# Applying the gate weight as expert results leave PSUM, and splitting the final adds between GpSimd and VectorE

## The reference, cut to what matters

```python
logits = x_flat @ gate_w.T
scores = jax.nn.softmax(logits, axis=-1)
_, topk_ids = jax.lax.top_k(scores, 2)                      # 8 experts, 2 per token
in_topk = jax.nn.one_hot(topk_ids, E, dtype=x.dtype).sum(axis=1)
w = scores * in_topk
gu = jnp.einsum('nh,eih->nei', x_flat, experts_gate_up)     # inner size 352
g, u = (gu[..., :I], gu[..., I:])
h = jax.nn.silu(g) * u
expert_out = jnp.einsum('nei,ehi->neh', h, experts_down)
out = jnp.einsum('neh,ne->nh', expert_out, w)
shared = jax.nn.silu(x_flat @ shared_gate_w.T) * (x_flat @ shared_up_w.T) @ shared_down_w.T
out = out + jax.nn.sigmoid(x_flat @ shared_expert_gate_w.T) * shared
x = x + jnp.tanh(g_ffn[1]) * out
```

## Time and profile before

| what | us |
|---|---|
| median of 3 runs | 1013.73 |
| lowest and highest run | 1010.68, 1014.83 |
| the profiled execution | 1013.72 |
| its span, first to last instruction | 1011.6 |
| TensorE busy | 944.7 |
| VectorE busy | 578.4 |
| ScalarE busy | 482.1 |
| GpSimd busy | 582.9 |

### The profile page before, as it was taken

One profiled execution on the slowest core, in us unless ns is written; L12 is line 12 of the kernel. 1 busy time (PEld: TensorE's weight loads), 2 busy tenths in 40 slices (PEclk: granted clock), 3 DMA queues, 4 the chain that ended last, 5 costly groups with the idle time before them and its releaser, 6 DMA issues. The chain is left out here.

```text
span 1011.6 us, 21397 instructions
## 1 busy us (share of the span) xinstructions
PE 944.7 (93%) x7715; PEld 537.0 (53%) x7716; DVE 578.4 (57%) x1698; ACT 482.1 (48%) x661; POOL 582.9 (58%) x620
## 2 busy tenths in 40 slices
PE   6989999999996997988999999998899999999994
PEld 3654444444464553644444444456456577777753
DVE  4867888888743123876888888837443222222226
ACT  2437777877843111326778788753301122222210
POOL 3468999999933900368999999961036222222210
PEclk9978999999997998998999999999999999999998
DMA  9581837364002160465243434111912212222143
GB/s 302 193 230 37 231 65 222 73 193 94 9 23 84 42 218 10 120 158 133 53 110 64 116 65 116 33 49 39 339 47 90 70 53 63 63 63 63 53 158 112
DMA packets 87988, 107.56 MB, mean 106 GB/s; under 512 B 10528, under 2 KB 70520, under 8 KB 87896
## 3 DMA queue, kind: packets, MB, share of 16 engines
q1 hardware_dynamic: 77192, 85.08, 30.4%
q0 software_dynamic: 4848, 14.70, 4.3%
q10 hardware_dynamic: 5856, 6.56, 2.1%
HBM read 76.92 MB, written 29.38 MB: 105 GB/s over the span
## 5 line engine op out<-in xcount | busy, mean ns | idle before, releaser
L616 ACT ACTIVATE pT<-ps 128x1024 f32<-128x1024 f32 x256 | 248.4, 1022 | 97.8 <-PE ps L488 97.5
L658 POOL TENSOR_TENSOR xT<-nmax,xT 128x512 f32<-128x512 f32 x192 | 195.5, 1040 | 20.6 <-DVE nmax L556 20.3
L658 POOL TENSOR_TENSOR s<-nmax,s 128x512 f32<-128x512 f32 x192 | 196.4, 1040 | 16.6 <-DVE nmax L556 12.4
L556 DVE CUSTOM_DVE_ANT_0 s<-ps,bias 128x512 f32<-128x512 f32 x256 | 166.1, 689 | 45.0 <-PE ps L475 43.8
L556 DVE CUSTOM_DVE_ANT_0 xT<-ps,bias 128x512 f32<-128x512 f32 x256 | 166.5, 689 | 41.6 <-PE ps L475 32.8
L475 PE MATMUL ps<-ks,qs 97*128 97x512 bf16 (+1 forms) x512 | 162.4, 397 | 10.7 <-DMA ks<-qk_scratch 4.5
L503 PE MATMUL ps<-pT,vq 128*32 128x512 f32 x1024 | 136.0, 608 | 2.4
L1186 POOL DMA_INDIRECT slots_out<-y,id x39 | 38.2, 980 | 128.6 <-DVE y L1513 128.6
L475 PEld LDWEIGHTS ps<-ks,qs 97*128 97x128 bf16 (+1 forms) x512 | 30.7, 98 | 130.3 <-DVE nmax L556 64.0
L1265 PE MATMUL ps<-gu,xgT 128*128 x312 | 98.8, 460 | 0.7 <-ACT xgT L1349 0.7
L488 PEld LDWEIGHTS ps<-ident,xT 64*128 64x128 f32 x2048 | 71.5, 143 | 29.2 <-issue 28.5
(11 more groups left out here) (173 smaller groups left out, 1179.5 us busy)
## 6 DMA issues: line engine op xcount, KB each, us to landing
bias<-in_bias SPq DMA_DIRECT2D x16, 1024.0 KB, 5.8
qk_scratch<-parts SPq DMA_DIRECT2D x64, 128.0 KB
qs<-qk_scratch SPq DMA_DIRECT2D x32, 192.0 KB, 3.4
ks<-qk_scratch SPq DMA_DIRECT2D x32, 192.0 KB, 4.0
gu<-in_gate_up SPq DMA_DIRECT2D x8, 704.0 KB, 9.7
slots_in<-zeros POOLq DMA_DIRECT2D x4, 1280.0 KB, 7.1
xg<-slots_in SPq DMA_DIRECT2D x39, 130.0 KB, 2.1
qk_scratch<-parts ACTq DMA_DIRECT2D x32, 128.0 KB
```

What stands on the lines that cost most here:

```text
L556: nc.vector.tensor_tensor_reduce(at.s[m % 4][:, qt, :], sb.ps[:, ring_bank(tile_place[u - 1 + hg * 64]), :], at.bias[:, j if per_head_bias ...
L616: nc.scalar.activation(at.pT[:, slot(m // HG, m % HG), 2 * half:2 * half + 2, :], sb.ps[:, 2 + 2 * half:4 + 2 * half, :], ACT.Exp).then_in ...
L658: nc.gpsimd.tensor_tensor(s, at.nmax[:, m % 4, qt:qt + 1].to_broadcast([P, S]), s, ALU.subtract).then_inc(pool_less_max, 1)
```

## The change

- **The weight travels with the row.** Before the scatters of each choice, GpSimd copies the 16 columns of m.w for that choice into word D + 1 of the rows of sb.tok. keep_id copies two words (row number and weight), and m.id grows to 128 x 4 x 2.
- **The weight is applied in keep_y.** The copy from PSUM becomes a tensor_scalar multiplication by the column m.id[:, u, 1].
- **GpSimd adds the two results of a batch.** Behind its last scatter it waits for both loads of a batch and adds sb.tok to yg in one tensor_tensor of 128x1024, for each of the four batches.
- **VectorE adds the sum in one operation.** expert_add is one tensor_tensor of 128x1024 per batch and waits for y_summed instead of the loads.
- **Order on VectorE.** expert_add of batch 0 now stands behind the first product of block (1,3) and that of batch 1 behind the second, ahead of the third product and of shared_add of (1,2). Batches 2 and 3 stay where they were. SP's stores wait for y_added of b + 1.

```diff
             for b in range(B):
-                sp.wait_ge(y_added, 2 * QT * (b + 1))
+                sp.wait_ge(y_added, b + 1)
                 sp.wait_ge(x_added, TT + QT * (b + 1))
...
                     nc.gpsimd.iota(sb.tok[:, :, D].bitcast(I32), pattern=[[P, TT]], base=N,
                                    channel_multiplier=1).then_inc(rows_named, 1)
-                    pool.wait_ge(rows_named, 3)
+                nc.gpsimd.tensor_copy(sb.tok[:, :, D + 1], m.w[:, c, :]).then_inc(rows_named, 1)
+                pool.wait_ge(rows_named, 3 + 2 * c)
                 for t in range(TT):
...
-                nc.gpsimd.tensor_copy(m.id[:, u:u + 1], m.xg[:, u, D:D + 1].bitcast(U32)).then_inc(id_kept, 1)
+                nc.gpsimd.tensor_copy(m.id[:, u, :], m.xg[:, u, D:D + 2].bitcast(U32)).then_inc(id_kept, 1)
...
             for it in range(ST // 4):
                 body(it, it == 0, it == ST // 4 - 1)
+            for b in range(B):
+                pool.wait_ge(y_loaded[b], 16 * 2)
+                rows = slice(QT * b, QT * (b + 1))
+                nc.gpsimd.tensor_tensor(m.yg[1][:, rows, :], m.yg[0][:, rows, 0:D], m.yg[1][:, rows, :],
+                                        ALU.add).then_inc(y_summed, 1)
...
-            def shared_prod(half, b):
+            def shared_prod(half, b, ready=0):
                 for i in range(SC):
...
                     nc.vector.tensor_tensor(hidden(half, b, i)[rows], m.g[rows, k % 2, :],
                                             sb.ps[rows, bank, :], ALU.mult).then_inc(s_prod, 1)
+                    if i < ready:
+                        expert_add(i)
...
                 dve.wait_ge(x_added, b * QT + QT)
-                dve.wait_ge(y_loaded[b], 16 * 2)
-                for c in range(2):
-                    for q in range(QT):
-                        t = b * QT + q
-                        if c == 1:
-                            dve.wait_ge(y_added, 2 * QT * b + q + 1)
-                        nc.vector.scalar_tensor_tensor(sb.x[:, t, :], m.yg[c][:, t, 0:D], m.w[:, c, t:t + 1],
-                                                       sb.x[:, t, :], ALU.mult, ALU.add).then_inc(y_added, 1)
+                dve.wait_ge(y_summed, b + 1)
+                rows = slice(QT * b, QT * (b + 1))
+                nc.vector.tensor_tensor(sb.x[:, rows, :], sb.x[:, rows, :], m.yg[1][:, rows, :],
+                                        ALU.add).then_inc(y_added, 1)
...
-                nc.vector.tensor_copy(m.y[:, u, :], sb.ps[:, 6 + u % 2, 0:D]).then_inc(y_kept, 1)
+                nc.vector.tensor_scalar(m.y[:, u, :], sb.ps[:, 6 + u % 2, 0:D], m.id[:, u, 1:2].bitcast(F32), None,
+                                        ALU.mult).then_inc(y_kept, 1)
...
             for n in range(1, len(late_blocks)):
-                shared_prod(*late_blocks[n])
+                half, b = late_blocks[n]
+                shared_prod(half, b, EARLY if n == 1 else 0)
                 shared_add(*late_blocks[n - 1])
-                if n == 1:
-                    for b in range(EARLY):
-                        expert_add(b)
                 dve.wait_ge(x_added, TT + (EARLY + n) * QT)
                 expert_add(EARLY + n - 1)
 
             expert_add(B - 1)
-            dve.wait_ge(y_added, 2 * TT)
+            dve.wait_ge(y_added, B)
             shared_add(*late_blocks[-1])
```

More of the change, by code:

```diff
@@ L1060, in mixture_phase @@
     id_kept, rows_named = sem("id_kept"), sem("rows_named")
-    y_added = sem("y_added")
+    y_summed, y_added = sem("y_summed"), sem("y_added")
     out_done = sem("out_done")
@@ L1186, in scatter_y @@
                 pool.indirect_dma_start(
-                    out=scr.ys, out_offset=bass.IndirectOffsetOnAxis(ap=m.id[:, u:u + 1], axis=0),
+                    out=scr.ys, out_offset=bass.IndirectOffsetOnAxis(ap=m.id[:, u, 0:1], axis=0),
                     in_=m.y[:, u, :], in_offset=None).then_inc(y_stored[u], 16)
@@ L1735, in build @@
                     m.xg = buf("xg", [P, 4, DW], F32)
-                    m.id = buf("id", [P, 4], U32)
+                    m.id = buf("id", [P, 4, 2], U32)
                     m.xgT = buf("xgT", [P, 2, DC, P], F32)
```

## The result

The changed kernel took 1002.18 us (median of 4 runs, 1000.65 to 1003.39) against 1012.53 before; the ratio is 0.9889, with a 95% interval of 0.9867 to 0.9911. The profiled execution took 1002.56 us, its span is 1000.8. Two later comparisons of the same pair gave 0.9896 (0.9868 to 0.9923) and 0.9906 (0.9874 to 0.9938). It is faster, by 1%. The recorded ratio is not the quotient of the two medians, which would be 0.9898; with the ratio the gain is 11.2 us, by the medians 10.4, and the interval covers both.

A forecast was written before the change was run, and what follows sets the result against it. VectorE's final adds were taken to bound the end; its end moving from 1008.23 to 999.04 gains 9.2 us, making the span 1002.4 and, with 2.1 outside it, 1004.5. Range 1001.3 to 1006.5, or to 1008.0 with two rivals.

The forecast's parts named there:

- What bounds: End of the kernel: VectorE holds it before the change; afterwards TensorE's last matmul, one shared_add and the store do.
- The final adds: VectorE's end: four additions of 128x1024 at 1.21 us replace 32 small ones taking 12.79 us; two move into idle time.
- GpSimd's sums: Four new GpSimd additions at the end, 2357 ns each, ready before VectorE wants them, with at least 1.7 us to spare.
- Turns: Possible mutual exclusion of GpSimd's sums and VectorE's adds; the end would stay, GpSimd's margin falling from 3.4 to about 2 us.
- part 2: The forecast's section on GpSimd's batch sums at the end, including load waits, the early store and possible waiting between engines.
- The first store: Batch 0's store, issued at about 985.6 instead of 997.06, could delay the last loads by about 1.5 us.
- The weight: keep_y in the expert loop: multiplication instead of copy, +0.06 us each, 2.3 us over 39 tiles, costing nothing.
- The scatter: Weight copies and a wait before the scatters: about 1.0 us ahead of the xg loads, hidden by 5 us of cover.
- (a): At the end, VectorE stays last because its new adds are slower or held: 1005.7, up to 1007; chance 0.08.
- (b): At the end, GpSimd's sums come late, batch 3's after 996: end 3.1 us later than forecast, 1007.6; chance 0.04.
- (d): Expert loop: multiplication or two-column id copy enters its cycle; 0.24 us per tile would eat the gain; chance 0.05.

The follow-up runs named there:

- no_ahead: The changed kernel with the adds of batches 0 and 1 left behind shared_add of block (1,2), as in the kernel before; ratio to before 0.9898.
- order_only: The kernel before with only the small expert adds of batches 0 and 1 moved behind the first two products of block (1,3); ratio 0.9916.
- weight_only: The changed kernel without GpSimd's sums, in the order of before, with 32 small VectorE adds; only the weight is moved; ratio to before 0.9978.
- sum_twice: The changed kernel with GpSimd making each batch's sum twice, first into a buffer nobody reads; ratio to before 0.9976.

## Why the prediction held, and where its size was off

**What bounds.** Right: VectorE held the end, and TensorE holds it now, 3.90 us ahead of the span's end where I had 3.89 (0.52 + 3.37).

**The final adds.** 1.21 forecast, 1.22 measured (no_ahead). By itself the move brings 6.2, GpSimd's sums with fewer and larger operations bring 8.1 without it, and both 9.2, because TensorE is last after that.

**GpSimd's sums.** 2357 ns forecast, 2352 measured where no add meets them. Turns were open; they were taken in the sequence that part 2 weighed. In the clock of before (1.63 later) batch 0's add ended at 986.8 where that sequence had 986.9, batch 1's at 990.1 (990.5), batch 3's sum at 992.3 (992.9) and the third product at 990.8 (991.2). VectorE wanted that last sum at about 995. The first store went out at 985.19 and took 4.9 us to land, against 2.9 for the median. The 1.5 us by which I had it hold up the last loads did not show: the last two took 8.7 and 8.9 us from issue to landing (8.6 and 8.9 before), and batch 3's sum began at 989.3 in the clock of before, where the loads alone gave 989.1.

**The weight.** 484 ns forecast 0.48; 2.4 us of VectorE's time, nothing on the path (195.18 to 195.18).

**The scatter.** I had 0.7 us for the first choice. The copy took 0.21 and the wait 0.59, but the first scatter stands 37.68 us into the last part against 37.62: before, the indirect DMA began 0.9 us behind its release anyway, and the new wait lies in that time. The last scatter is 0.4 later; TensorE's first turn is at 95.3 in both.

**The size.** The last part went as forecast: 9.17 us where I had 9.2. The step that failed is the one from the span to the time: "The profiled execution took 1013.72, 2.1 more than its span, and the median of the runs is 1013.73, so both give 1004.5", and with it the low end of the range. It took two terms for constants.

- The part ahead of the last part. It took 706.41 us in after and 708.04 in before, 1.63 less, and 704.12 to 710.44 over all 13 profiles.
- The time outside the span, which is a run's time less its span. It was 2.06 to 2.19 us in every run of before and of the two kernels with 32 small adds (order_only, weight_only), and 1.69 to 1.83 in every run of the others: the change brings 0.37 us there, which no row of the profile shows. Why is open.

Together they are 2.0 us and make up, within the rounding of the spans, the 1.94 us between the forecast of 1004.5 and the profiled execution of 1002.56. The ratio applied to the median of its own comparison gives 0.9889 x 1012.53 = 1001.29, a gain of 11.2, a hair below my range, which began at 1001.3. The range reached 3.2 below the forecast, as far as three runs of one kernel had scattered, and left out that both sides of a comparison do: the median of before itself was 1012.5, 1015.3, 1012.3 and 1014.1 in four comparisons. It should have begun about 2 us lower.

What the profiles account for is 9.17 + 0.37 = 9.5 us, a ratio of 0.9906. All three intervals hold it, but no measured ratio is above it, so whether the rest of the 11.2 us is scatter alone stays open, as said under the unchanged part.

**The rivals.** (a) did not come about, though two adds were held to twice their time, since both had cover. (b) was made real by sum_twice. I priced it at 3.1; it was 5.8, because the turns were not in the price: 3.1 and three adds at 0.86 on GpSimd give 5.7. The late product was not on the path, since the last add waited for GpSimd until 998.54, when TensorE had ended at 997.44. (d): the loop did not move by 0.01 us per tile.

## What to carry to other kernels

Where a chain ends on an engine that adds up results, look first for work in it that was ready long before and stands behind something late: moving half of the expert adds into idle time brought 6.2 of the 9.2 us without one faster operation. Then merge small operations, and stop when the next engine is last; here about 1.1 us of VectorE's saving lay beyond that point (its adds end 10.3 us earlier in the last part, the end comes 9.2 earlier). Measure such a gain from a fixed event near the change. Here that repeated to 0.05 us where whole runs scatter by several, save in two profiles where a lower clock had made one stretch 1.7 us longer; so look at the stretches, and not only at the sum.

## What the runs showed of the hardware

A VectorE tensor_tensor with both inputs in SBUF and a GpSimd tensor_tensor exclude each other, as far as these rows go: 1.22 us alone, 2.37 to 3.29 when started inside a sum, and the sum behind it 0.4 to 0.9 longer. GpSimd memsets did not hold it (1.22). A product with one input in PSUM took its usual 0.69 us inside a sum (982.06). The Trainium skill (SBUF — State Buffer, Who interferes with whom) says that a VectorE instruction with two SBUF inputs contends with a GpSimd one that reads SBUF and not with one that only writes. These rows agree in both halves. They do not say that two SBUF inputs are needed: the cast of the earlier trace rows has one and was held.

A scalar_tensor_tensor of 128x256 in SBUF repeats every 0.395 us, a tensor_tensor of the same size every 0.335.

An unchanged stretch of some 700 us differed by up to 6.3 us between executions of these kernels. In the two profiles of before, the granted clock of its three parts differed by 0.02 to 0.03, while the mean over the whole span was 0.971 in both. What makes the clock fall where it does stays open.
